# The one-hots of the edge stage made on ScalarE as a clipped distance, in place of VectorE's comparison

## The chip, the cores and the metric

The kernel runs on one core of one Trainium2 chip. The metric is the device time of one execution in microseconds (us), as the median of several runs; less is better. The engines are named as the profile names them: PE is TensorE (matrix products, with PEld for its weight loads), DVE is VectorE, ACT is ScalarE, POOL is GpSimd, SP is SyncE, which only issues DMAs here.

## What is computed

The program is one layer of a graph network on 12,500 nodes with 256 features and 212,500 edges, sorted by their receiving node (`row`). Cut to what matters:

```python
h = relu(layernorm(x))
xn = layernorm(h) * ln_w + ln_b
w_phys = (silu(rbf @ w1 + b1) @ w2 + b2) * cutoff[:, None]
Q, K, V = xn @ wq + bq, xn @ wk + bk, xn @ wv + bv      # 8 heads of 32
q_e, k_e, v_e = Q[row], K[col], V[col]
scores = sum(q_e * k_e, per head) / sqrt(32) * cutoff[:, None]
attn = softmax(scores, axis=1)                          # over the 8 heads of one edge
combined = xn[col] * w_phys + gate * attn * v_e
aggr = segment_sum(combined, row)
out = x + h + aggr @ wo + bo
```

## The kernel before, in words

The program has three stages. The first (`prep`) makes the node tables, sorts the edges into buckets of 128 receiving nodes, computes `w_phys` for each edge and writes one record per edge to memory. The last (`finish`) multiplies the sums by `wo`. Between them stands the edge stage (`edges`), the only place that the change touches.

The edge stage works in **units** of 256 edge slots (two columns j of 128 edges, one edge per partition), UNITS of them, 880 in all. A record (`REC` = 260 floats) holds an edge's 256 weights, its cutoff (`R_CUT`), the number 0 to 127 of its receiving node in its bucket (`R_LOC`) and the number of its sending node (`R_DST`). Buffers for records, gathered rows and one-hots are DEPTH = 8 units deep. For each unit u:

- SP loads the records of unit u (L1010), once the last readers of unit u - 8's buffer are done: `physical`, `weigh` and `select` on VectorE (L1007 to L1009).
- GpSimd gathers the 768 floats (K, V, xn) of each sending node by two indirect DMAs (L1029). It runs GATHER_AHEAD = 5 units ahead in its own count and waits until TensorE has aggregated unit u - 8 and until the record is there.
- VectorE's `select` (L1191) makes the one-hots of two units at once: it compares the column numbers 0 to 127 (`iota_bf`, bf16) with `R_LOC` of each edge. The result `ohb` (`uonehot_bf`) is a matrix of edges by nodes of the bucket, one 1 in each row.
- TensorE's `turn` (L1103) transposes the two one-hots of a unit into PSUM, and ScalarE's `evacuate` (L1046) copies them to `uonehotT` as float32. `query` (L1111) multiplies them by the bucket's queries, which gives each edge its Q row.
- ScalarE's `widen` (L1052) copies `ohb` to float32 (`uonehot`) for the aggregation.
- VectorE multiplies queries by keys (`query_key`, L1198, each unit), weights by xn (`physical`, L1203), reduces over the heads (`score`, L1210), scales (`weigh`, L1215), takes the maximum (`maximum`, L1220), inverts and normalises after ScalarE's exponentials (L1225, L1230), and weighs the values (`attend`, L1236). All of these but `query_key` work on a **pair** of units.
- ScalarE's `exponent` (L1060) makes the four exponentials of a pair.
- TensorE's `aggregate` of unit u - 3 (LAG = 3) multiplies the float32 one-hots by the two products (L1131, L1134) and sums them in PSUM, `renew_next` (L1115) zeroes the next bank, and ScalarE's `keep` (L1070) copies the sums out.

The order of each engine is written out by hand: a function `unit` per engine, called for unit 0, 1, 2 and so on, in which `ahead(fn, n, ...)` issues the step fn of unit u + n. An engine executes its own order strictly; between engines there are only semaphores. VectorE's `unit` in the kernel before, for odd u:

```python
                else:
                    score(u, k, i, first)
                    weigh(u, k, i, first)
                    maximum(u, k, i, first)
                    ahead(select, SELECT_AHEAD - 1, u, k, i, first, last)
```

ScalarE's `unit` issues `evacuate` and `widen` of unit u + 2, for odd u `exponent`, then `keep` of unit u - 3. TensorE's issues `aggregate(u - 3)`, `turn(u + 3)`, `query(u + 2)`, `renew_next(u - 3)`; for even u it first loads bucket numbers into registers.

## Time and profile before

| | |
|---|---|
| median of 3 runs | 5721.61 us (5720.52 to 5729.41) |
| the profiled execution | 5727.87 us |
| its span | 5726.1 us |
| PE busy | 5242.1 us, 92% |
| DVE busy | 4458.7 us, 78% |
| POOL busy | 4114.1 us, 72% |
| ACT busy | 3117.6 us, 54% |
| mean TensorE clock granted | 0.987 of full speed |

A busy time is the sum over the whole span, so it mixes the three stages. The edge stage takes the stretch from about 2590 us to about 5590 us. In it, an engine's idle time before a group of instructions is given with what released it ("<-"); "issue" is time in which it waited for nothing that the profile shows. Matmuls are pipelined and their ends are modelled, so the distance between two starts says more about PE than its busy share.

### The profile page before, as it was taken

What the parts mean: (1) busy time and instruction counts of PE and PEld (TensorE: products, weight loads), DVE (VectorE), ACT (ScalarE), POOL (GpSimd) and SP (SyncE); (2) the same over time, 40 slices, a digit from 0 to 9 for tenths busy, and PEclk for the clock granted to TensorE, in tenths of its full rate; (3) what the DMA queues carried; (4) which work ended last, traced back from release to release, by engine and by line L of the source; (5) the groups of instructions that cost most, each with busy time, mean ns of one, the idle gap of its engine ahead of it and who ended that gap; (6) DMA issues with size and microseconds to landing.
All of it is one profiled execution on the core that took longest, in us unless ns stands there. A gap on an engine that the chain in (4) does not pass through costs nothing. (4 is left out here: it accounts for less than half of the span.)

```text
span 5726.1 us, 115218 instructions
## 1 busy us (share of the span) xinstructions
PE 5242.1 (92%) x24352; PEld 3838.2 (67%) x24353; DVE 4458.7 (78%) x7861; ACT 3117.6 (54%) x9962; POOL 4114.1 (72%) x3476
## 2 busy tenths in 40 slices
PE   3889999999999999996899999999999999999999
PEld 3556666666666666664666666666666666666667
DVE  8889976666655554226899999999999999999995
ACT  4546565666666666563455555555555555555553
POOL 1567777777777777675777777777777777777770
PEclk9989999999999999997999999999999999999999
DMA  6234354444444444438999999999999999999955
GB/s 196 90 109 150 121 169 165 156 134 157 165 155 142 150 166 159 142 125 299 312 307 303 305 308 304 303 305 303 308 305 306 307 307 304 304 306 306 308 185 180
DMA packets 584396, 1306.11 MB, mean 228 GB/s; under 512 B 81246, under 2 KB 384134, under 8 KB 582961
## 3 DMA queue, kind: packets, MB, share of 16 engines
q0 software_dynamic: 221536, 881.08, 44.2%
q1 hardware_dynamic: 311796, 345.48, 20.4%
q10 hardware_dynamic: 50850, 77.03, 3.7%
q8 instruction: 95, 1.56, 0.1%
q14 instruction: 119, 0.97, 0.1%
HBM read 1024.15 MB, written 324.38 MB: 236 GB/s over the span
## 5 line engine op out<-in xcount | busy, mean ns | idle before, releaser
L1029 POOL DMA_INDIRECT ukvx<-kvx_table,urec x1760 | 2302.3, 1308 | 705.0 <-issue 640.5
L339 POOL DMA_INDIRECT records<-rows,slot_i x1660 | 1743.9, 1051 | 682.8 <-issue 468.5
L694 PE MATMUL w_ps<-w2s,hid 128*128 128x256 f32 x6656 | 1553.9, 387 | 51.3 <-DVE rows L608 51.1
L694 PEld LDWEIGHTS w_ps<-w2s,hid 128*128 128x128 f32 x6656 | 1249.9, 193 | 375.3 <-issue 156.5
L608 DVE TENSOR_TENSOR rows<-w_ps,b2b 128x512 f32<-128x512 f32 x832 | 571.3, 687 | 744.1 <-PE w_ps L694 743.9
L1131 PE MATMUL ag_ps<-ukvx,uonehot 128*128 128x256 f32 x3520 | 987.3, 403 | 153.5 <-DVE ukvx L1203 78.2
L1111 PE MATMUL uq_ps<-aggr,uonehotT 128*128 x3520 | 974.9, 400 | 0.3 <-issue 0.3
L808 ACT ACTIVATE hid<-hid_ps,b1t 128x512 f32<-128x512 f32 x832 | 525.4, 682 | 820.9 <-PE hid_ps L683 806.2
L1134 PE MATMUL ag_ps<-ukvx,uonehot 128*128 128x256 f32 x3520 | 906.5, 380 | 1.0 <-DVE ukvx L1236 1.0
L1060 ACT ACTIVATE uexp<-uscores,umax 128x8 f32<-128x8 f32 x1760 | 507.5, 289 | 649.2 <-DVE umax L1220 649.1
L1131 PEld LDWEIGHTS ag_ps<-ukvx,uonehot 128*128 128x128 f32 x3520 | 600.1, 190 | 372.2 <-issue 273.9
L1046 ACT ACTIVATE uonehotT<-turn_ps 128x256 f32<-128x256 bf16 x880 | 328.6, 373 | 831.8 <-PE turn_ps L1103 826.7
L829 ACT ACTIVATE rows<-rows 128x256 f32<-128x256 f32 x1664 | 706.9, 504 | 66.5 <-DVE rows L608 66.3
L1134 PEld LDWEIGHTS ag_ps<-ukvx,uonehot 128*128 128x128 f32 x3520 | 670.9, 191 | 93.6 <-DVE ukvx L1236 1.8
L1111 PEld LDWEIGHTS uq_ps<-aggr,uonehotT 128*128 128x128 f32 x3520 | 601.1, 190 | 90.3 <-issue 0.6
L1198 DVE TENSOR_TENSOR ukvx<-uq_ps,ukvx 128x512 f32<-128x512 f32 x880 | 601.3, 683 | 0.5 <-PE uq_ps L1111 0.5
L1210 DVE TENSOR_REDUCE uscores<-ukvx 128x32 f32<-128x1024 f32 x440 | 536.7, 1220 | 50.5 <-DVE ukvx L1198 20.6
L1236 DVE TENSOR_TENSOR ukvx<-ukvx,uexp 128x1024 f32<-128x1024 f32 x440 | 539.2, 1225 | 45.7
L1203 DVE TENSOR_TENSOR ukvx<-urec,ukvx 128x1024 f32<-128x1024 f32 x440 | 534.6, 1215 | 11.3 <-DMA ukvx<-kvx_table,urec 11.1
L1070 ACT ACTIVATE aggr<-ag_ps x880 | 510.0, 580 | 2.7 <-ACT aggr L1070 1.6
L683 PE MATMUL hid_ps<-rT,w1d 64*128 64x512 f32 x1664 | 472.8, 645 | 26.7 <-ACT hid L808 20.6
L441 DVE TENSOR_TENSOR_SCAN cs_ps<-eq,run 128x512 f32<-128x512 bf16 (+1 forms) x396 | 405.8, 1025 | 28.4 <-DVE run L449 11.1
(174 smaller groups left out, 4629.6 us busy)
## 6 DMA issues: line engine op xcount, KB each, us to landing
urec<-records SPq DMA_DIRECT2D x880, 260.0 KB, 6.3
rbf_in<-in_edge_attr SPq DMA_DIRECT2D x207, 256.0 KB, 3.0
kvx_table<-kvx ACTq DMA_DIRECT2D x10, 3456.0 KB, 14.5
ukvx<-kvx_table,urec POOLq DMA_INDIRECT x1760, 5.9
records<-rows,slot_i POOLq DMA_INDIRECT x1661, 2.1
records<-kvx SPq DMA_DIRECT2D x1, 13000.0 KB
aggr<-query_table SPq DMA_DIRECT2D x7, 1792.0 KB, 20.1
fbase<-x_plus_h SPq DMA_DIRECT2D x14, 896.0 KB, 7.2
```

Source lines behind the costliest of these rows:

```text
L339: pool.indirect_dma_start(recs, bass.IndirectOffsetOnAxis(ap=slot_i[:, q, t:t + 1], axis=0), rows[:, q, t, :], None).then_inc(scattered[q] ...
L608: dve.tensor_tensor(rows[:, q, 2 * j:2 * j + 2, 0:H], w_ps[j % 2][:], b2b[:].unsqueeze(1).to_broadcast([P, 2, H]), ALU.add).then_inc(s["w_ ...
L694: m = pe.matmul(w_ps[j % 2][:, h, :], hid[:, k % 2, c, h, j * P:(j + 1) * P], w2s[:, c, :], start=(h == 0 and c == 0), stop=(c == 1), skip ...
L829: m = act.activation(rows[:, q, t, 0:H], rows[:, q, t, 0:H], ACT.Copy, scale=rows[:, q, t, R_CUT:R_CUT + 1])
L1029: pool.indirect_dma_start(kvx[:, k, j, :], None, table, bass.IndirectOffsetOnAxis(ap=rec[:, k, j, R_DST:R_DST + 1].bitcast(I32), axis=0), ...
L1111: m = pe.matmul(q_ps[k % 3][:, j, :], ohT[:, k % 4, j, :], aggr[:, bass.ds(buckets[j] + QLAG, 1), :].rearrange("p a f -> p (a f)"), start= ...
L1131: pe.matmul(to[j], oh[:, k, j, :], kvx[:, k, j, 2 * H:3 * H], start=False, stop=False, skip_group_check=True)
L1134: m = pe.matmul(to[j], oh[:, k, j, :], kvx[:, k, j, H:2 * H], start=False, stop=(j == 1), skip_group_check=True)
L1198: dve.tensor_tensor(kvx[:, k, :, 0:H], q_ps[k % 3][:], kvx[:, k, :, 0:H], ALU.mult).then_inc(s["qk_done"], 1)
L1203: dve.tensor_tensor(both, pair(rec, k)[:, :, 0:H], both, ALU.mult).then_inc(s["phys_done"], 2)
L1210: dve.tensor_reduce(sc[:, q], pair(kvx, k - 1)[:, :, 0:H].rearrange("p r (h d) -> p r h d", h=NH), AX_X, ALU.add).then_inc(s["scored"], 2)
L1236: dve.tensor_tensor(values, values, ex[:, q].unsqueeze(3).to_broadcast([P, 4, NH, HD]), ALU.mult).then_inc(s["av_done"], 2)
```

## The change

`select` is gone from VectorE. ScalarE makes the one-hots of all units in two steps, in bf16 and in place. `spread` writes the distance |R_LOC - column| with the function Abs (one instruction of 128x128 for each of the two columns j, since the bias is one number per partition). `pick` writes Relu(1 - distance), which is 1 where the distance is 0 and 0 elsewhere (one instruction of 128x256 per unit, its bias from a new tile `one` that VectorE sets once). In ScalarE's `unit`, `spread` of unit u + 5 and `pick` of unit u + 4 stand behind `exponent` and ahead of `keep`. TensorE's `turn`, ScalarE's `widen` and SP's record load wait for the new semaphore `picked` where they waited for `onehot_ready`. At the start ScalarE makes the distances of units 0 to 4 and the one-hots of units 0 to 3 ahead of its first `evacuate`.

```diff
@@ -929,6 +929,7 @@
         kvx = sb("ukvx", [P, DEPTH, 2, TAB])
         iota_bf = sb("uiota_bf", [P, P], BF16)
         ohb = sb("uonehot_bf", [P, DEPTH, 2, P], BF16)
+        one = sb("uone", [P, 1])
         ident_bf = sb("uident_bf", [P, P], BF16)
         oh = sb("uonehot", [P, DEPTH, 2, P])
         ohT = sb("uonehotT", [P, 4, 2, P])
@@ -941,7 +942,7 @@
         ag_ps = ps("ag_ps", [P, SUMS, H])
 
         s = {n: sem("u_" + n) for n in (
-            "zeroed", "narrow", "blank", "rec_waited", "onehot_ready", "widened", "turned", "ohT_ready", "qe_done",
+            "zeroed", "narrow", "blank", "rec_waited", "one_ready", "spread", "picked", "widened", "turned", "ohT_ready", "qe_done",
             "qk_done", "phys_done", "scored", "weighted", "max_done", "exp_ready", "recip_done", "shared",
             "av_done", "ag_waited", "ag_done", "kept", "q_waited", "named")}
         rec_in = [sem(f"u_rec_in{k}") for k in range(DEPTH)]
@@ -949,7 +950,7 @@
         q_in = sem("u_q_in")
         kvx_in = [sem(f"u_kvx_in{k}") for k in range(DEPTH)]
         TURNS = UNITS // DEPTH
-        GATHER_AHEAD, SELECT_AHEAD, TURN_AHEAD, OUT_AHEAD, ASK_AHEAD = 5, 4, 3, 2, 2
+        GATHER_AHEAD, SPREAD_AHEAD, TURN_AHEAD, OUT_AHEAD, ASK_AHEAD = 5, 5, 3, 2, 2
         rec_v = recs.rearrange("(u j p) f -> u p j f", p=P, j=2)
         q_v = queries.rearrange("(b p) f -> p b f", p=P)
 
@@ -1006,7 +1007,7 @@
                 if not first:
                     sp.wait_ge(s["phys_done"], u - (DEPTH - 1))
                     sp.wait_ge(s["weighted"], u - (DEPTH - 1))
-                    sp.wait_ge(s["onehot_ready"], u - (DEPTH - 1))
+                    sp.wait_ge(s["picked"], u - (DEPTH - 1))
                 sp.dma_start(rec[:, k], rec_v[u] if isinstance(u, int) else rec_v[bass.ds(u, 1)].rearrange("a p j f -> p (a j) f")).then_inc(rec_in[k], 16)
                 if first and k == 2:
                     ask_first(0, q_first[0])
@@ -1045,8 +1046,21 @@
                     act.wait_ge(s["qe_done"], u - 3)
                 act.activation(ohT[:, k % 4], turn_ps[:, 0:2, :], ACT.Copy).then_inc(s["ohT_ready"], 1)
 
+            def spread(u, k, i, first):
+                act.wait_ge(rec_in[k], i * 16 + 16)
+                if not first:
+                    act.wait_ge(s["widened"], u - (DEPTH - 1))
+                    act.wait_ge(s["turned"], u - (DEPTH - 1))
+                for j in range(2):
+                    m = act.activation(ohb[:, k, j, :], iota_bf[:], ACT.Abs, scale=-1.0, bias=rec[:, k, j, R_LOC:R_LOC + 1])
+                m.then_inc(s["spread"], 1)
+
+            def pick(u, k, i, first):
+                act.wait_ge(s["spread"], u + 1)
+                act.activation(ohb[:, k], ohb[:, k], ACT.Relu, scale=-1.0, bias=one[:, 0:1]).then_inc(s["picked"], 1)
+
             def widen(u, k, i, first):
-                act.wait_ge(s["onehot_ready"], u + 1)
+                act.wait_ge(s["picked"], u + 1)
                 if not first:
                     act.wait_ge(s["ag_done"], u - (DEPTH - 1))
                 act.activation(oh[:, k], ohb[:, k], ACT.Copy).then_inc(s["widened"], 1)
@@ -1071,6 +1085,12 @@
 
             act.activation(half_asked[:], half_bucket[:, HPAD:HPAD + HALVES], ACT.Copy).then_inc(s["named"], 1)
             bucket_of = [None] * 4
+            act.wait_ge(s["narrow"], 2)
+            act.wait_ge(s["one_ready"], 1)
+            for k in range(SPREAD_AHEAD):
+                spread(k, k, 0, True)
+                if k:
+                    pick(k - 1, k - 1, 0, True)
             for k in range(OUT_AHEAD):
                 evacuate(k, k, 0, True)
                 widen(k, k, 0, True)
@@ -1082,6 +1102,8 @@
                 ahead(widen, OUT_AHEAD, u, k, i, first, last)
                 if k % 2:
                     exponent(u, k, i, first)
+                ahead(spread, SPREAD_AHEAD, u, k, i, first, last)
+                ahead(pick, SPREAD_AHEAD - 1, u, k, i, first, last)
                 if not (first and k < LAG):
                     keep(u - LAG, bucket_of[k % 2 * 2])
             turns(act, unit)
@@ -1096,7 +1118,7 @@
         @block.tensor
         def _(pe):
             def turn(u, k, i, first):
-                pe.wait_ge(s["onehot_ready"], u + 1)
+                pe.wait_ge(s["picked"], u + 1)
                 if not (first and k == 0):
                     pe.wait_ge(s["ohT_ready"], u)
                 for j in range(2):
@@ -1182,15 +1204,6 @@
             def pair(tile, k):
                 return tile[:, k:k + 2].rearrange("p k j e -> p (k j) e")
 
-            def select(u, k, i, first):
-                for n in range(2):
-                    dve.wait_ge(rec_in[k + n], i * 16 + 16)
-                if not first:
-                    dve.wait_ge(s["widened"], u - (DEPTH - 2))
-                    dve.wait_ge(s["turned"], u - (DEPTH - 2))
-                dve.tensor_tensor(pair(ohb, k), iota_bf[:].unsqueeze(1).to_broadcast([P, 4, P]),
-                                  pair(rec, k)[:, :, R_LOC:R_LOC + 1].to_broadcast([P, 4, P]), ALU.is_equal).then_inc(s["onehot_ready"], 2)
-
             def query_key(u, k, i, first):
                 q = k % 2
                 dve.wait_ge(s["qe_done"], u + 1)
@@ -1235,13 +1248,11 @@
                 values = pair(kvx, k - 1)[:, :, H:2 * H].rearrange("p r (h d) -> p r h d", h=NH)
                 dve.tensor_tensor(values, values, ex[:, q].unsqueeze(3).to_broadcast([P, 4, NH, HD]), ALU.mult).then_inc(s["av_done"], 2)
 
+            dve.memset(one[:], 1.0).then_inc(s["one_ready"], 1)
             dve.tensor_copy(ident_bf[:], ident[:]).then_inc(s["narrow"], 1)
             dve.tensor_copy(iota_bf[:], iota1[:]).then_inc(s["narrow"], 1)
             for k in range(GATHER_AHEAD):
                 dve.memset(kvx[:, k], 0.0).then_inc(s["blank"], 1)
-            dve.wait_ge(s["narrow"], 2)
-            for k in range(0, SELECT_AHEAD, 2):
-                select(k, k, 0, True)
             dve.memset(zeros_bf[:], 0.0).then_inc(s["zeroed"], 1)
             dve.memset(ag_ps[:], 0.0).then_inc(s["zeroed"], 1)
             for k in range(GATHER_AHEAD, DEPTH):
@@ -1258,7 +1269,6 @@
                     score(u, k, i, first)
                     weigh(u, k, i, first)
                     maximum(u, k, i, first)
-                    ahead(select, SELECT_AHEAD - 1, u, k, i, first, last)
             turns(dve, unit)
             U = UNITS
             before = (U - 1, DEPTH - 1, TURNS - 1, False)
```

**ScalarE, one odd unit and its neighbour in the steady loop.** Rows are instructions in ScalarE's order; L1052 is `widen`, L1060 the four exponentials, L1070 `keep`. Before:

```order
L1052 ACTIVATE uonehot<-uonehot_bf 128x256
L1056 REGISTER_ALU
L1058 REGISTER_ALU
L1060 ACTIVATE uexp,usum<-uscores,umax 128x8 x4
L1070 REGISTER_ALU x2
L1070 ISA
L1070 REGISTER_ALU
L1070 ISA
L1070 ACTIVATE aggr<-ag_ps 128x512
```

With the change (L1066 is `widen`, L1074 the exponentials, L1055 `spread`, L1060 `pick`, L1084 `keep`):

```order
L1066 ACTIVATE uonehot<-uonehot_bf 128x256
L1070 REGISTER_ALU
L1074 ACTIVATE uexp,usum<-uscores,umax 128x8 x4
L1055 ACTIVATE uonehot_bf<-uiota_bf,urec 128x128 x2
L1059 REGISTER_ALU
L1060 ACTIVATE uonehot_bf<-uonehot_bf,uone 128x256
L1084 REGISTER_ALU x2
L1084 ISA
L1084 REGISTER_ALU
L1084 ISA
L1084 ACTIVATE aggr<-ag_ps 128x512
```

Three instructions stand between the exponentials and `keep`; in an even unit the same three follow `widen` directly.

**VectorE, from the end of one pair to the next, in the steady loop.** L1220 is `maximum`, L1191 `select`, L1198 `query_key`, L1203 `physical`. Before:

```order
L1210 TENSOR_REDUCE uscores<-ukvx 128x32
L1215 SCALAR_TENSOR_TENSOR uscores<-uscores,urec 128x32
L1220 TENSOR_REDUCE umax<-uscores 128x4
L1187 ISA
L1191 TENSOR_TENSOR uonehot_bf<-uiota_bf,urec 128x512
L1196 REGISTER_ALU
L1198 TENSOR_TENSOR ukvx<-uq_ps,ukvx 128x2x256
L1203 TENSOR_TENSOR ukvx<-urec,ukvx 128x4x256
```

With the change (L1233 is `maximum`, L1211 `query_key`, L1216 `physical`):

```order
L1223 TENSOR_REDUCE uscores<-ukvx 128x32
L1228 SCALAR_TENSOR_TENSOR uscores<-uscores,urec 128x32
L1233 TENSOR_REDUCE umax<-uscores 128x4
L1209 REGISTER_ALU
L1211 TENSOR_TENSOR ukvx<-uq_ps,ukvx 128x2x256
L1216 TENSOR_TENSOR ukvx<-urec,ukvx 128x4x256
```

`query_key` of the next unit follows the maximum; nothing else has moved on VectorE.

## Rows read from the trace of the kernel before

**Rows 1.** The page: busy times over the span, and two groups of its part 5.

```profile
PE 5242.1 (92%) x24352; PEld 3838.2 (67%) x24353; DVE 4458.7 (78%) x7861; ACT 3117.6 (54%) x9962; POOL 4114.1 (72%) x3476
...
L829 ACT ACTIVATE rows<-rows 128x256 f32<-128x256 f32 x1664 | 706.9, 504 | 66.5 <-DVE rows L608 66.3
...
L1198 DVE TENSOR_TENSOR ukvx<-uq_ps,ukvx 128x512 f32<-128x512 f32 x880 | 601.3, 683 | 0.5 <-PE uq_ps L1111 0.5
```

**Rows 2.** Stage table: window, length, busy us per engine, clock, DMA share, GB/s.

```profile
4000.00:4500.00 500.00, 457.63 (x2221) 347.77 (x2220) 453.87 (x742) 257.86 (x1037) 390.77 (x297) 1.00 0.92 307
```

**Rows 3.** Instruction groups, window 2700 to 5500 us: busy us, mean ns, idle before.

```profile
L1029 POOL DMA_INDIRECT ukvx<-kvx_table,urec x1658 | 2176.8, 1313 | 625.7 <-issue 600.5 <-PE ag_ps L1134 22.7 <-DMA urec<-records 2.5
L1131 PE MATMUL ag_ps<-ukvx,uonehot 128*128 128x256 f32 x3312 | 926.4, 402 | 147.3 <-DVE ukvx L1203 76.4 <-ACT uonehot L1052 70.8 <-issue 0.2
...
L1198 DVE TENSOR_TENSOR ukvx<-uq_ps,ukvx 128x512 f32<-128x512 f32 x828 | 565.8, 683 | 0.0
...
L1203 DVE TENSOR_TENSOR ukvx<-urec,ukvx 128x1024 f32<-128x1024 f32 x414 | 503.0, 1215 | 4.6 <-DMA ukvx<-kvx_table,urec 4.6
...
L1060 ACT ACTIVATE uexp<-uscores,umax 128x8 f32<-128x8 f32 x1656 | 477.5, 289 | 599.8 <-DVE umax L1220 599.8
...
L1191 DVE TENSOR_TENSOR uonehot_bf<-uiota_bf,urec 128x512 bf16<-128x512 bf16 x414 | 286.5, 692 | 36.7 <-DMA urec<-records 0.2
```

**Rows 4.** Waits, same window: engine, line, releaser; total us, times, longest.

```profile
ACT uonehotT L1046 <- PE turn_ps L1103: 758.3, 415, 3.2
...
PE turn_ps L1103 <- DVE uonehot_bf L1191: 90.4, 309, 2.1
```

**Rows 5.** VectorE's timeline across one boundary of pairs: start us, length us.

```profile
4003.75 0.19 DVE L1220 TENSOR_REDUCE umax<-uscores 128x4 f32<-128x32 f32 x1
4004.08 0.69 DVE L1191 TENSOR_TENSOR uonehot_bf<-uiota_bf,urec 128x512 bf16<-128x512 bf16 x1
4004.69 0.68 DVE L1198 TENSOR_TENSOR ukvx<-uq_ps,ukvx 128x512 f32<-128x512 f32 x1
4005.29 1.22 DVE L1203 TENSOR_TENSOR ukvx<-urec,ukvx 128x1024 f32<-128x1024 f32 x1
```

**Rows 6.** VectorE's timeline in the start of the edge stage.

```profile
2606.58 0.69 DVE L1191 TENSOR_TENSOR uonehot_bf<-uiota_bf,urec 128x512 bf16<-128x512 bf16 x1 [9.16 <-DMA urec<-records]
...
2614.32 0.63 DVE L1198 TENSOR_TENSOR ukvx<-uq_ps,ukvx 128x512 f32<-128x512 f32 x1
```

**Rows 7.** ScalarE's timeline: two exponentials of 8 columns in a row.

```profile
4004.27 0.28 ACT L1060 ACTIVATE uexp<-uscores,umax 128x8 f32<-128x8 f32 x1
...
4004.56 0.28 ACT L1060 ACTIVATE uexp<-uscores,umax 128x8 f32<-128x8 f32 x1
```

**Rows 8.** ScalarE's timeline in the first stage: four instructions of L829 merged.

```profile
1501.18 1.70 ACT L829 ACTIVATE rows<-rows 128x256 f32<-128x256 f32 x4
```

**Rows 9.** TensorE's timeline: the first matmuls of three units in a row.

```profile
3999.62 1.13 PE L1131 MATMUL ag_ps<-ukvx,uonehot 128*128 128x256 f32 x4 [0.22 <-ACT uonehot L1052]
...
4002.50 1.11 PE L1131 MATMUL ag_ps<-ukvx,uonehot 128*128 128x256 f32 x4
...
4006.41 1.12 PE L1131 MATMUL ag_ps<-ukvx,uonehot 128*128 128x256 f32 x4 [0.23 <-ACT uonehot L1052]
```

**Rows 10.** GpSimd's timeline: three gathers in a row.

```profile
4003.93 1.01 POOL L1029 DMA_INDIRECT ukvx<-kvx_table,urec  x1 [0.30 <-issue]
4005.38 2.00 POOL L1029 DMA_INDIRECT ukvx<-kvx_table,urec  x1 [0.44 <-issue]
4007.69 1.41 POOL L1029 DMA_INDIRECT ukvx<-kvx_table,urec  x1 [0.30 <-issue]
```

**Rows 11.** Stage table in short windows, columns as in rows 2.

```profile
4002.00:4004.00 2.00, 2.00 (x11) 1.68 (x11) 1.64 (x4) 0.47 (x3) 1.39 (x3) 1.00 1.08 417
...
2652.00:2660.00 8.00, 5.98 (x31) 4.52 (x30) 5.52 (x9) 3.47 (x14) 6.07 (x6) 1.00 1.02 380
```

**Rows 12.** DMA issues, window 2700 to 5500 us: count, KB each, us to landing.

```profile
urec<-records SPq DMA_DIRECT2D x828, 260.0 KB, 6.3
```

## The prediction

> **What bounds the kernel now.** On the page [rows 1] TensorE is busy 92% of the span and ScalarE 54%, which invites the reading that TensorE is the bound and that ScalarE has room to give. A page adds up three stages, so the next view is the stage table, and in it the edge stage alone [rows 2]: in 500 us VectorE is busy 453.87, TensorE 457.63, GpSimd 390.77, ScalarE 257.86, the clock is at its full level and the DMA engines are at 0.92. Four resources are near their end, so busy shares can't name the one that sets the pace; what an engine waits for can. The groups of the window 2700 to 5500 [rows 3] hold 414 pairs of units, so a pair takes 2800 / 414 = 6.76 us. VectorE's idle time before its instructions is released by nobody else: `query_key` 0.0 us, `physical` 4.6 us on a gather, `select` 36.7 us of which 0.2 us is a DMA. What is left of its idle time is the latency between its own dependent steps. TensorE waits for VectorE (`turn` on `select`, 90.4 us), ScalarE waits 758.3 us for TensorE [rows 4] and 599.8 us for the maximum [rows 3]. All chains lead to VectorE, so **VectorE's own sequence is the bound**, and its length per pair is the time per pair. `query_key` is issued 880 times in all [rows 1], so there are 440 pairs.
>
> **What VectorE loses.** In the timeline [rows 5] `select` starts at 4004.08 and the next `query_key` at 4004.69, so it takes 0.61 us of the sequence (its 0.69 us overlap the next start). Between the end of the maximum (4003.94) and `select` there are 0.14 us; on average this idle is 36.7 / 414 = 0.09 us [rows 3]. Whether it goes too is not to be seen in the trace: `query_key` also has waits of its own to be cleared after the maximum was issued, as `select` had. The ends are 0.61 (the gap stays) and 0.70 (it goes). I take 0.61, since every VectorE step that follows a small reduction shows such a gap. That gives 6.76 - 0.61 = 6.15 us per pair and 440 x 0.61 = **-268 us**; the other end is 440 x 0.70 = -308 us.
>
> **The start of the stage.** VectorE stood 9.16 us in the second `select` until a record had landed, then cleared more buffers, and began `query_key` at 2614.32 [rows 6]. Now ScalarE waits for the records, also for that of unit 4, before its first `evacuate`, while VectorE goes on clearing. One comes earlier and the other later. The ends are -8 us (2614.32 - 2606.58, all of VectorE's clearing goes ahead) and +3 us (the new work of five units, estimated below, comes on top). The first queries are not there much before 2614, so I take 0. The new memset of one column and the two selects of the start lie in the same cover.
>
> **What ScalarE gains.** Per unit two instructions of 128x128 and one of 128x256, each with its bias from SBUF. Four instructions of 128x256 with such an operand take 1.70 us [rows 8] and one takes 0.504 [rows 1], so they follow each other by (1.70 - 0.504) / 3 = 0.40 us. With 8 columns the starts lie 4004.56 - 4004.27 = 0.29 us apart [rows 7] (the read of the accumulator fits into that), so 128 columns lie between 0.29 and 0.40; by columns 0.34. Per pair: 4 x 0.34 + 2 x 0.40 = 2.16 us. ScalarE is busy 257.86 / 500 x 6.76 = 3.49 us per pair now [rows 2], so it comes to 5.65 of 6.15 us. It fits, and it fits because its idle time lies in two waits per pair: before `evacuate` (758.3 / 414 = 1.8 us) and before the exponentials (599.8 / 414 = 1.45 us) [rows 3, 4]. About 1.1 us of new work falls before each. The first 1.1 us use up most of the 1.45 us left before the exponentials, so these start on time. The second 1.1 us delay the `evacuate` behind the exponentials, and with it TensorE's `query` of two units later. VectorE has never waited for a query there (0.0 us [rows 3]), so there is reserve, of unknown size. I cost ScalarE at nothing; without this cover each 0.1 us per pair is 44 us.
>
> The Trainium skill (ScalarE: Activation LUTs, Rules for kernel authors) speaks against this change: relu and the like belong on VectorE, not on ScalarE. Rows 3 agree as to the work, 0.69 us on VectorE against 2.16 us estimated on ScalarE. By that rule the sum would be a loss, which is my rival on the other side; by the rows the cheap engine is the one that is full.
>
> **What TensorE can do.** Without a wait inside, a unit takes 4002.50 - 3999.62 = 2.88 us; the next took 3.91 us [rows 9]. Of the difference, the wait for `select` goes: `pick` of a unit is issued well before its `turn`. The idle time before the first matmul, 147.3 / 414 = 0.36 us per pair [rows 3], comes with the loading of bucket numbers into registers (the releasers named had long been done) and may stay. TensorE's floor is then 2 x 2.88 + 0.36 = 6.12 us, just under VectorE's 6.15. It is late next, by nearly nothing.
>
> **What GpSimd can do.** Its gathers follow each other with gaps of 0.30 to 0.44 us and look like a bound of their own [rows 10]. A gather takes 1.01 us, but 2.00 when it begins with `physical` and 1.41 within `attend`; the mean is 1.313 us [rows 3]. With gaps of 0.30 four gathers take 4 x 1.61 = 6.45 us per pair. But the stretching follows VectorE: a gather that starts inside such an instruction goes on when it ends, so gathers and pairs are locked in phase. In a shorter pair the same gather starts later inside `physical` and loses less. It loses 0.99 us beside `physical` now and needs to lose 6.45 - 6.15 = 0.30 us less. So GpSimd should follow at 6.15 us. If it doesn't, it is the bound at 6.45.
>
> The Trainium skill (SBUF — State Buffer, Who interferes with whom) says that a VectorE instruction with two SBUF inputs contends with a GpSimd instruction that reads SBUF. The two products agree, with 2.00 and 1.41 us against 1.01; `select` has two SBUF inputs as well, and the gather that ran beside it took 1.01 [rows 5, 10]. By that rule GpSimd would regain up to 0.4 us per pair, as much as a gather loses within `attend`, and my rival (a) below would drop out. The row shows nothing to regain, so I leave (a) its chance.
>
> **What the DMA engines can do.** Their share of 0.92 times 6.76 is 6.22 us per pair, if a share of 1 were the limit. But a share holds time in which two queues' packets overlap, and 307 GB/s [rows 2] is not the most: 380 over 8 us, 417 over 2 us [rows 11]. 6.15 us per pair need 307 x 6.76 / 6.15 = 337 GB/s. A record takes 6.3 us to land [rows 12], and under more load longer. I expect a few tenths more, within the distance that SP and GpSimd run ahead.
>
> **The sum.** The profiled execution took 5727.9 us; less 268 that is 5459.9 us. It lies 6.3 us above the median of the runs shown, so the median should be about 5454 us.
>
> **Rivals.** *Another resource at its end, faster by less.* (a) GpSimd holds at 6.45 us per pair: 440 x 0.31 = -136 us, 5586 us. For it: it has no long idle time now. Against it: VectorE almost never waited for a gather, though GpSimd has no reserve to catch up with if it were the slower. Chance 0.17. (b) DMA at a share of 1, 6.22 us: -238 us, 5484 us, or TensorE keeps half of the 1.03 us that its longer unit has over the shorter [rows 9], 2 x 2.88 + 0.52 = 6.28 us: -211 us, 5511 us. Chance 0.13.
>
> *ScalarE becomes the bound, slower.* The mechanism is the strict order on ScalarE behind the exponentials: `spread`, `pick` and `keep` stand ahead of the next `evacuate`, and VectorE's reciprocal waits for the next exponentials. It decides from the point at which the six new instructions of a pair cost more than 6.76 - 3.49 = 3.27 us, 0.55 each. If none overlaps its neighbour and each first waits for a semaphore, they cost up to 0.504 + 0.1 (as between VectorE's dependent steps) = 0.6, 3.6 us per pair, and the pair takes 7.09: 440 x 0.33 = +145 us, 5867 us. Half of that is as likely, 5790 us. Against it: ScalarE's neighbours overlap by 0.1 us wherever the trace shows them, also after a release. Chance 0.09.
>
> *It does not do what it says:* VectorE's pace was set from outside and only looked full, so that the freed 0.61 us turn into a wait for gathers or queries. 5722 us. The 4.6 and 0.0 us of waits [rows 3] speak against it. Chance 0.04.
>
> **How the numbers follow.** VectorE (with TensorE beside it) as the bound at 6.06 to 6.2 us per pair has a chance of 0.57, and gives 5408 to 5480 us. With (b) it is 0.70, with (a) 0.87. The range has to hold 0.8: from 5405 us (the gap goes too, and 3 us of the start) to 5620 us, which takes in (a) with a margin for slower landings. Left out are the slower case, the case of no change and the space between. A measurement of this kernel can tell about 0.2% from no change. Faster by more: 0.57 + 0.13 + 0.17 = 0.87; within: 0.04; slower: 0.09.
>
> **What would show it.** In the groups of the window 2700 to 5500 there should be about 455 pairs. VectorE's `query_key` should still be preceded by no idle time released by others. TensorE's wait for the one-hots should be gone. `spread` should show a mean near 0.39 us and `pick` near 0.50, and ScalarE a busy share near 0.9. The gather's mean should be below 1.313 us, and its waits for TensorE no longer than now. The DMA rate should be near 337 GB/s. I am wrong if `physical` waits for gathers by tenths of a us per pair (then it is (a) or (b)), if the reciprocal waits for the exponentials or `turn` for ScalarE (then it is ScalarE), or if `query_key` waits for the queries (then it is TensorE).

## The result, and the profile after

| | before | with the change |
|---|---|---|
| median | 5725.51 us (4 runs) | 5507.36 us (4 runs, 5505.26 to 5509.57) |
| span of the profiled execution | 5726.1 us | 5503.4 us |
| ratio | | 0.9618, 95% interval 0.9602 to 0.9635 |

The change makes the kernel 3.8% faster, 218 us, where 268 were forecast. The page of the changed kernel, the line that answers to the first of [rows 1]:

```profile
PE 5147.0 (94%) x24352; PEld 3858.7 (70%) x24353; DVE 4196.1 (76%) x7422; ACT 3928.7 (71%) x12602; POOL 3871.3 (70%) x3476
```

VectorE has 262.6 us less to do and ScalarE 811 us more. The stage table, as [rows 2]:

```profile
4000.00:4500.00 500.00, 481.34 (x2409) 382.81 (x2410) 445.92 (x723) 427.61 (x1606) 376.46 (x322) 1.00 0.96 333
```

ScalarE went from 258 to 428 busy us in 500; the DMA rate rose from 307 to 333 GB/s. The groups of the window 2700 to 5300 us (busy us, mean ns, idle before, as [rows 3]; the new lines are L1211 `query_key`, L1216 `physical`, L1055 `spread`, L1060 `pick`, L1074 exponentials, L1030 gathers):

```profile
L1030 POOL DMA_INDIRECT ukvx<-kvx_table,urec x1664 | 1947.4, 1170 | 652.5 <-issue 621.8 <-PE ag_ps L1156 15.9 <-DMA urec<-records 14.8
...
L1211 DVE TENSOR_TENSOR ukvx<-uq_ps,ukvx 128x512 f32<-128x512 f32 x832 | 571.5, 687 | 45.2 <-issue 30.8 <-PE uq_ps L1133 14.3
...
L1055 ACT ACTIVATE uonehot_bf<-uiota_bf,urec 128x128 bf16<-128x128 bf16 x1664 | 566.8, 389 | 5.9 <-DMA urec<-records 5.8
...
L1216 DVE TENSOR_TENSOR ukvx<-urec,ukvx 128x1024 f32<-128x1024 f32 x416 | 506.7, 1218 | 31.3 <-DMA ukvx<-kvx_table,urec 29.0
...
L1074 ACT ACTIVATE uexp<-uscores,umax 128x8 f32<-128x8 f32 x1664 | 479.7, 289 | 374.0 <-DVE umax L1233 371.4 <-issue 2.5
L1060 ACT ACTIVATE uonehot_bf<-uonehot_bf,uone 128x256 bf16<-128x256 bf16 x833 | 413.0, 496 | 0.0
```

416 pairs in 2600 us are 6.25 us per pair, against 6.76 before and 6.15 forecast. `spread` takes 389 ns and `pick` 496, as estimated. The gather's mean fell from 1313 to 1170 ns. VectorE now has idle time that others end: 29.0 us on gathers where it had 4.6, and 14.3 us on queries, of which 14.0 lie before 2800 us.

The mean hides that most pairs (267 of the last 419) are shorter than 6.15 us. VectorE's timeline over two boundaries of pairs (start us, length us):

```profile
4008.31 0.19 DVE L1233 TENSOR_REDUCE umax<-uscores 128x4 f32<-128x32 f32 x1
4008.49 0.69 DVE L1211 TENSOR_TENSOR ukvx<-uq_ps,ukvx 128x512 f32<-128x512 f32 x1
...
4014.43 0.19 DVE L1233 TENSOR_REDUCE umax<-uscores 128x4 f32<-128x32 f32 x1
4014.92 0.69 DVE L1211 TENSOR_TENSOR ukvx<-uq_ps,ukvx 128x512 f32<-128x512 f32 x1 [0.31 <-issue]
```

At an ordinary boundary the gap between the maximum and `select` (0.14 us in [rows 5]) went together with `select`: `query_key` starts where the maximum ends. At one boundary in four, where VectorE's loop of 8 units turns (jumps back to its start), 0.31 us stand open instead. Taking the distance between the starts of every second `query_key` over the whole stage, the medians of the four pairs of a loop turn are

| us per pair (medians) | 1st | 2nd | 3rd | 4th | mean of all pairs after the 20th |
|---|---|---|---|---|---|
| before | 6.86 | 6.68 | 6.78 | 6.68 | 6.751 |
| with the change | 6.13 | 6.03 | 6.03 | 6.38 | 6.217 |

The first 20 pairs took 154.2 us before and 164.3 us after, so they gained nothing. These three things, the longer fourth pair, the difference between the mean and the medians, and the slow start, are what the experiments take apart.

### The profile page after: what moved, and what is told of

Its sections match the earlier page's. It is cut to its first block and busy times, and to the rows that moved or that the text cites. A ratio compares the mean times of both kernels' runs of the same rounds, so it can differ in the third digit from the quotient of the medians.

```text
span 5503.4 us, 117739 instructions
## 1 busy us (share of the span) xinstructions
PE 5147.0 (94%) x24352; PEld 3858.7 (70%) x24353; DVE 4196.1 (76%) x7422; ACT 3928.7 (71%) x12602; POOL 3871.3 (70%) x3476
## 5 line engine op out<-in xcount | busy, mean ns | idle before, releaser
L1030 POOL DMA_INDIRECT ukvx<-kvx_table,urec x1760 | 2058.7, 1170 | 737.6 <-issue 663.6
L1133 PE MATMUL uq_ps<-aggr,uonehotT 128*128 x3520 | 976.9, 400 | 88.4 <-issue 72.7
L1074 ACT ACTIVATE uexp<-uscores,umax 128x8 f32<-128x8 f32 x1760 | 507.3, 289 | 402.2 <-DVE umax L1233 399.7
L829 ACT ACTIVATE rows<-rows 128x256 f32<-128x256 f32 x1664 | 706.7, 504 | 66.7 <-DVE rows L608 66.7
L1133 PEld LDWEIGHTS uq_ps<-aggr,uonehotT 128*128 128x128 f32 x3520 | 602.4, 191 | 206.1 <-issue 155.2
L1211 DVE TENSOR_TENSOR ukvx<-uq_ps,ukvx 128x512 f32<-128x512 f32 x880 | 604.5, 687 | 76.1 <-PE uq_ps L1133 44.5
L1055 ACT ACTIVATE uonehot_bf<-uiota_bf,urec 128x128 bf16<-128x128 bf16 x1760 | 599.6, 389 | 43.3 <-DMA urec<-records 43.1
L1216 DVE TENSOR_TENSOR ukvx<-urec,ukvx 128x1024 f32<-128x1024 f32 x440 | 535.9, 1218 | 36.9 <-DMA ukvx<-kvx_table,urec 34.7
L1084 ACT ACTIVATE aggr<-ag_ps x880 | 508.6, 578 | 2.3 <-ACT aggr L1084 1.6
L1060 ACT ACTIVATE uonehot_bf<-uonehot_bf,uone 128x256 bf16<-128x256 bf16 x880 | 436.3, 496 | 0.0
```

Source lines behind the costliest of these rows:

```text
L829: m = act.activation(rows[:, q, t, 0:H], rows[:, q, t, 0:H], ACT.Copy, scale=rows[:, q, t, R_CUT:R_CUT + 1])
L1030: pool.indirect_dma_start(kvx[:, k, j, :], None, table, bass.IndirectOffsetOnAxis(ap=rec[:, k, j, R_DST:R_DST + 1].bitcast(I32), axis=0), ...
L1055: m = act.activation(ohb[:, k, j, :], iota_bf[:], ACT.Abs, scale=-1.0, bias=rec[:, k, j, R_LOC:R_LOC + 1])
L1133: m = pe.matmul(q_ps[k % 3][:, j, :], ohT[:, k % 4, j, :], aggr[:, bass.ds(buckets[j] + QLAG, 1), :].rearrange("p a f -> p (a f)"), start= ...
L1211: dve.tensor_tensor(kvx[:, k, :, 0:H], q_ps[k % 3][:], kvx[:, k, :, 0:H], ALU.mult).then_inc(s["qk_done"], 1)
```

## The experiments

All ratios are against the kernel before. The last two columns come from the one profiled execution of each kernel. Two executions of the same code can reach the edge stage some us apart (VectorE's first instruction of the stage came at 2579.8 us in the profile of the changed kernel, at 2588.5 in that of the kernel before and at 2592.7 in another, although the change does not touch what stands ahead). Differences below 10 us between medians are therefore read with the times inside the stage.

| kernel | median us | ratio (95% interval) | first 20 pairs us | mean of the rest us |
|---|---|---|---|---|
| changed kernel | 5507.4 | 0.9618 (0.9602 to 0.9635) | 164.3 | 6.217 |
| e_compare_back | 5667.6 | 0.9892 (0.9876 to 0.9909) | 166.9 | 6.575 |
| e_free_act | 5471.7 | 0.9559 (0.9543 to 0.9575) | 145.0 | 6.167 |
| e_half_records | 5497.8 | 0.9599 (0.9583 to 0.9615) | 160.2 | 6.195 |
| e_half_query | 5504.9 | 0.9605 (0.9589 to 0.9621) | 159.0 | 6.217 |
| e_all_light | 5458.4 | 0.9527 (0.9513 to 0.9542) | 143.2 | 6.136 |
| e_free_records | 5456.1 | 0.9529 (0.9515 to 0.9544) | 144.2 | 6.132 |
| e_busy_act | 5493.9 | 0.9591 (0.9577 to 0.9606) | 147.0 | 6.222 |
| e_act_beside | 5730.6 | 1.0005 (0.9996 to 1.0015) | 154.8 | 6.754 |
| e_keep_first | 5508.8 | 0.9615 (0.9600 to 0.9630) | 166.3 | 6.222 |
| e_spread_later | 5504.4 | 0.9608 (0.9594 to 0.9623) | 155.4 | 6.241 |
| e_branch_moved | 5488.2 | 0.9582 (0.9569 to 0.9595) | 164.8 | 6.169 |
| e_branch_load | 5476.9 | 0.9568 (0.9555 to 0.9581) | 159.5 | 6.163 |

### VectorE's comparison back, as work that nobody waits for

```diff
+            def compare(u, k, i, first):
+                dve.tensor_tensor(spare[:].rearrange("p k j e -> p (k j) e"), iota_bf[:].unsqueeze(1).to_broadcast([P, 4, P]),
+                                  marks[:].to_broadcast([P, 4, P]), ALU.is_equal)
...
                     maximum(u, k, i, first)
+                    compare(u, k, i, first)
```

> The changed kernel with VectorE's comparison back as work that nobody waits for: the same 128x512 bf16 instruction into a spare tile, from a constant, behind the maximum. If VectorE's sequence sets the pace, the pair gets 0.61 us back at least (to 6.64) and the time is 5507 + 0.53 to 0.61 x 440 = 5740 to 5775, or 5715 if the register-free form leaves a part of the gap out and slack elsewhere absorbs some. If TensorE or ScalarE had become the bound, less than half of it returns: below 5640.

It returned 160 us, less than the theory that it should confirm had said, and a little more than the other theory's bound. VectorE's timeline of this kernel says why (L1239 is the maximum, L1210 the comparison, L1217 `query_key`):

```profile
4006.51 0.18 DVE L1239 TENSOR_REDUCE umax<-uscores 128x4 f32<-128x32 f32 x1
4006.61 0.68 DVE L1210 TENSOR_TENSOR uspare<-uiota_bf,umarks 128x512 bf16<-128x512 bf16 x1
4007.21 0.68 DVE L1217 TENSOR_TENSOR ukvx<-uq_ps,ukvx 128x512 f32<-128x512 f32 x1
```

The comparison without waits starts 0.10 us after the start of the maximum and overlaps it by 0.08 us, so the gap of the kernel before is not there. `select` had four semaphore waits and read the record; the comparison has no wait and reads a constant. Which of the two made the gap no run separates. An ordinary pair takes 6.54 us by the medians, 0.51 more than 6.03. The fourth takes 6.54 too, only 0.16 more than 6.38: the comparison covers the open 0.31 us there. And the scatter is gone: in the changed kernel 47 pairs after the 20th are over 6% above the median and add 33 us, here one. VectorE's sequence sets the pace of nearly every pair in both kernels; the other disturbances show in the changed kernel and no longer when VectorE's own pair is about 0.5 us longer.

The same timeline shows what the comparison does to a gather that begins inside it:

```profile
4006.69 1.48 POOL L1032 DMA_INDIRECT ukvx<-kvx_table,urec  x1 [0.30 <-issue]
```

It takes 1.48 us in place of 1.01 (297 gathers begin inside it in the window 2700 to 5300 and take 1.47 us on average). In the kernel before `select` did the same:

```profile
4017.62 0.69 DVE L1191 TENSOR_TENSOR uonehot_bf<-uiota_bf,urec 128x512 bf16<-128x512 bf16 x1
...
4017.86 1.33 POOL L1029 DMA_INDIRECT ukvx<-kvx_table,urec  x1 [0.30 <-issue]
```

### The three suspects relieved, one by one and together

ScalarE unburdened: one-hots are made in the first turn of 8 units only, so later units use those of other edges.

```diff
-                ahead(spread, SPREAD_AHEAD, u, k, i, first, last)
-                ahead(pick, SPREAD_AHEAD - 1, u, k, i, first, last)
+                if first and k < DEPTH - SPREAD_AHEAD:
+                    spread(u + SPREAD_AHEAD, k + SPREAD_AHEAD, 0, True)
+                if first and k < DEPTH - SPREAD_AHEAD + 1:
+                    pick(u + SPREAD_AHEAD - 1, k + SPREAD_AHEAD - 1, 0, True)
...
-                pe.wait_ge(s["picked"], u + 1)
+                pe.wait_ge(s["picked"], u + 1 if first else DEPTH)
```

`widen` waits like `turn`, and the record load no longer waits for `picked`.

> The changed kernel, with ScalarE's spread and pick only in the first turn of 8 units; later units use those one-hots again, so the one-hots of all later units are not those of their edges. VectorE as changed, ScalarE unburdened as before the change. Records theory (VectorE paces at 6.03 us per pair, and what is missing to 6.03 is records and gathers that land late): within 15 us of the changed kernel's 5507. ScalarE theory (its 2 us of new work per pair delay the evacuations, and TensorE's turn and query behind them): 5400 to 5440. TensorE theory (tied with VectorE, its own register loads cost in each fourth pair): 5495 to 5507.

-36 us against the changed kernel, between the two forecasts. In the profile the first 20 pairs fall from 164.3 to 145.0 us and the rest from 6.217 to 6.167 us per pair (21 us).

Shorter records: from the second turn on the first 128 of the 256 weights are not loaded.

```diff
+                lo = 0 if first else H // 2
...
+                sp.dma_start(rec[:, k, :, lo:REC], src[:, :, lo:REC]).then_inc(rec_in[k], 16)
```

> The changed kernel, but from the second turn on the record load leaves out the first 128 of the 256 weights (260 floats become 132), so the physical product uses old weights there. DMA work per pair falls by 0.26 MB of 2.1 MB and records land sooner. Records theory: the disturbed pairs (some 0.09 us per pair) and the slow first 20 pairs (43 us over 6.03 each) mostly go, 5507 becomes 5425 to 5460. ScalarE and TensorE theories: 5495 to 5507.

-10 us, far less than the records theory had said. Late records alone are not all that is missing.

TensorE relieved: after the first turn only half of each unit's query products.

```diff
-                for j in range(2):
+                for j in range(2 if first else 1):
                     m = pe.matmul(q_ps[k % 3]
```

> The changed kernel, but after the first turn query multiplies only the first 128 edges of each unit, so the other half uses old query rows. TensorE saves about 0.85 us per pair. TensorE theory: each fourth pair falls from 6.38 to about 6.1 us and disturbed pairs are caught up sooner, 5460 to 5480. Records theory: 5490 to 5507, since VectorE's chain is as long. ScalarE theory: 5495 to 5507.

No difference that can be told, and the fourth pair stays at 6.34 us. Neither the pace nor the longer fourth pair comes from TensorE's query products.

All three together:

> The changed kernel with all three reliefs together: one-hots only in the first turn, half the weights loaded, half the query products (outputs are not the reference's). Only VectorE's own chain is left at its full length: 4 pairs in 6.13 + 6.03 + 6.03 + 6.34, 6.13 on average, 440 x 6.13 = 2697 us and about 2690 + 26 us from the start of the stage: about 80 us under the changed kernel's 2799, 5425 to 5440. Above 5450 something else holds VectorE that none of the three touches.

5458.4 us. The time was 18 us above the range and the pairs were as expected: 6.136 us on average against the 6.13 of the four medians, so nothing holds VectorE up after the start, and only the start's 143 us (20 x 6.13 would be 123) were more than I had allowed. What holds VectorE up there, none of the three reliefs shows. The first two reliefs without the third:

> The changed kernel with two of the three reliefs of the earlier run (one-hots only in the first turn, half the weights loaded), the query products whole. If TensorE has no part in what is missing to VectorE's chain: 5455 to 5463, as with all three (5458). If it has: 5467 to 5472, as with ScalarE relieved alone.

5456.1 us, as with all three, so TensorE's query products have no part in it. VectorE's `physical` in this kernel, window 2700 to 5300:

```profile
L1219 DVE TENSOR_TENSOR ukvx<-urec,ukvx 128x1024 f32<-128x1024 f32 x423 | 514.1, 1215 | 5.7 <-DMA ukvx<-kvx_table,urec 5.7
```

VectorE's wait for gathers is back at 5.7 us, where ScalarE's relief alone had left 13.5 and the changed kernel has 29.0. So the account is: from 5726 to 5456 us for VectorE's shorter sequence with everything else out of its way, 270 us; given back 36 us for ScalarE, and 16 us while the full records load beside it (51 us in all).

### What of ScalarE costs: its wait for records, or its being full

e_busy_act takes the kernel with one-hots in the first turn only and puts three instructions of the same kinds and sizes in place of `spread` and `pick` in every later unit, from a constant tile, with a wait for their own predecessors but for no record.

```diff
+            def beside(u, k, i):
+                act.wait_ge(s["beside"], u * 3 - (DEPTH * 3 - 3))
+                for j in range(2):
+                    act.activation(spare[:, j, :], ramp[:, j, :], ACT.Abs, scale=-1.0, bias=one[:, 0:1]).then_inc(s["beside"], 1)
+                act.activation(spare2[:], ramp[:], ACT.Relu, scale=-1.0, bias=one[:, 0:1]).then_inc(s["beside"], 1)
```

> The kernel with one-hots only in the first turn, plus on ScalarE in every later unit the three instructions of spread and pick at their place, from a constant tile into spare tiles: ScalarE is as full as in the changed kernel, but waits for no record. (One-hots of later units are not those of their edges.) Head-of-line theory (the 36 us between the changed kernel and ScalarE unburdened come from its wait for records ahead of the next evacuation): 5465 to 5480. Occupation theory (they come from ScalarE being 0.85 busy, so that a late pair isn't caught up): 5500 to 5512.

Neither theory alone: 5493.9 us, 22 us above ScalarE unburdened and 14 below the changed kernel. The two halves lie at different places. The first 20 pairs take 147.0 us, as with ScalarE unburdened (145.0); the rest takes 6.222 us per pair, as in the changed kernel (6.217). So at the start it is the wait for records, and from then on it is ScalarE being full. (The profiled execution of this kernel is the slowest of its four, 10 us above the median; the two columns are from it.) In the later part VectorE waits longer for gathers, not for queries. Its waits in the window 2800 to 5300 (total us, times, longest):

```profile
DVE ukvx L1229 <- DMA ukvx<-kvx_table,urec: 26.0, 51, 1.8
```

This wait is 8.6 us with ScalarE unburdened and 24.3 us in the changed kernel; for queries VectorE waits under 1 us in all three. The chain at the start can be read in the changed kernel's timeline (L1055 `spread`, L1125 `turn`, L1133 `query`, L1211 `query_key`):

```profile
2628.91 0.69 ACT L1055 ACTIVATE uonehot_bf<-uiota_bf,urec 128x128 bf16<-128x128 bf16 x2 [11.34 <-DMA urec<-records]
...
2630.38 0.37 ACT L1047 ACTIVATE uonehotT<-turn_ps 128x256 f32<-128x256 bf16 x1
...
2630.89 0.37 PE L1125 MATMUL turn_ps<-uident_bf,uonehot_bf 128*128 128x128 bf16 x2 [9.82 <-ACT uonehotT L1047]
...
2631.53 2.07 PE L1133 MATMUL uq_ps<-aggr,uonehotT 128*128 x4 [0.26 <-issue]
...
2633.63 0.69 DVE L1211 TENSOR_TENSOR ukvx<-uq_ps,ukvx 128x512 f32<-128x512 f32 x1 [11.39 <-PE uq_ps L1133]
```

A record for five units ahead is late, ScalarE stands 11.34 us in `spread`, the evacuation of three units ahead stands behind it although its input is long there, TensorE waits 9.82 us for the evacuation, and VectorE 11.39 us for the queries. In the kernel before, `select` asked for the same record later in the order, and ScalarE never stood for one.

The same three instructions beside the kernel before, with `select` in place:

> The kernel before with VectorE's select as it was and on ScalarE the same three instructions per unit as work that nobody waits for. If ScalarE's idle time covers 2 us per pair at 6.75 us per pair: the kernel before's time within 8 us, so 5720 to 5737. If the occupation of ScalarE costs by itself: 5745 or more.

A ratio of 1.0005, and 6.754 us per pair against 6.751. ScalarE was 396 us busy in 500 there:

```profile
4000.00:4500.00 500.00, 458.00 (x2222) 347.98 (x2221) 453.84 (x741) 395.65 (x1480) 391.01 (x297) 1.00 0.92 306
```

So 2 us of new work per pair on ScalarE cost nothing at 6.75 us per pair, and 22 us in all at 6.2 us. The idle time before the exponentials is the reserve that differs: with this work it is 1.36 us per pair at 6.75, and 374.0 / 416 = 0.90 us in the changed kernel. It may be that a pair that comes late for another reason is caught up by less in each of the next pairs. That this is how it acts is an inference from the two runs, and how a full ScalarE makes gathers late is not shown: the profile names no releaser for most of GpSimd's idle time.

### Two other orders on ScalarE

`spread` and `pick` behind `keep` in place of ahead of it:

```diff
-                ahead(spread, SPREAD_AHEAD, u, k, i, first, last)
-                ahead(pick, SPREAD_AHEAD - 1, u, k, i, first, last)
                 if not (first and k < LAG):
                     keep(u - LAG, bucket_of[k % 2 * 2])
+                ahead(spread, SPREAD_AHEAD, u, k, i, first, last)
+                ahead(pick, SPREAD_AHEAD - 1, u, k, i, first, last)
```

> The changed kernel with spread and pick behind keep in ScalarE's unit in place of ahead of it. The record's arrival then holds back the evacuation only, no longer the keep. If keep behind late one-hots were part of the loss: 5490 or less. Head-of-line theory (the evacuation of unit u+3 behind the wait for record u+5 is what costs, and it stays behind it here): 5500 to 5512.

Nothing changes (5508.8 us), as the head-of-line theory had it: it is not `keep` behind `spread` that matters. That leaves the evacuation, and the `widen` behind it.

`spread` four units ahead in place of five (`SPREAD_AHEAD` 4, with `pick` of the same unit right behind it):

> The changed kernel with spread only 4 units ahead in place of 5, and pick directly behind it, so ScalarE asks for each record one unit (3 us) later, but waits once more for its own result in each unit. Head-of-line theory: ScalarE's waits for records at the start of the stage (28 us in the first 160 us) shrink, and so does the slow start (20 pairs in 164 us): 5475 to 5495. If ScalarE's occupation alone is what costs, the added wait makes it worse: 5510 to 5540.

5504.4 us, within neither range and no difference that can be told. It has both effects: the first 20 pairs take 155.4 us, 9 less, and the rest 6.241 us per pair, 10 us more in all. ScalarE's idle time before the exponentials falls by half:

```profile
ACT uexp L1074 <- DVE umax L1232: 179.8, 398, 1.8
```

This is from its waits in the window 2800 to 5300 us. `pick` now waits for `spread` to end before each start.

### The longer fourth pair

VectorE's steps in the same order, but its loop turns behind `query_key` of unit 0 in place of ahead of it:

```diff
             def unit(u, k, i, first, last):
-                query_key(u, k, i, first)
                 if k % 2 == 0:
...
                     maximum(u, k, i, first)
-            turns(dve, unit)
+                ahead(query_key, 1, u, k, i, first, last)
+            query_key(0, 0, 0, True)
+            turns(dve, unit)
```

> The changed kernel, with VectorE's steps in the same order but the loop turning (once in four pairs) after query_key of unit 0 in place of before it, so that 0.69 us of work runs while the branch is taken. Branch theory (the comparison used to run while the loop turned; without it 0.31 us per turn lie open before query_key): each fourth pair falls from 6.34 to about 6.05 us, and 107 turns x 0.3 = 30 us go: 5470 to 5485. If the longer fourth pair comes from TensorE or from late gathers: 5500 to 5510.

5488.2 us, 19 less than the changed kernel; the intervals of the two ratios (0.9569 to 0.9595, 0.9602 to 0.9635) don't touch. The fourth pair falls from 6.38 to 6.07 us. In the groups of the window 2700 to 5300 the 30.8 us of "issue" before `query_key` are gone:

```profile
L1211 DVE TENSOR_TENSOR ukvx<-uq_ps,ukvx 128x512 f32<-128x512 f32 x837 | 576.0, 688 | 17.3 <-PE uq_ps L1133 14.3
```

In the kernel before the loop turned behind `select`, whose 0.69 us covered it: between `select` and `query_key` there is no idle time at that boundary either.

```profile
4010.76 0.69 DVE L1191 TENSOR_TENSOR uonehot_bf<-uiota_bf,urec 128x512 bf16<-128x512 bf16 x1
...
4011.37 0.69 DVE L1198 TENSOR_TENSOR ukvx<-uq_ps,ukvx 128x512 f32<-128x512 f32 x1
```

With `select` gone it turned behind the maximum, 0.19 us long. The measured gain is a little under the 22 to 37 us expected; in the profile it is 0.048 us per pair, 20 us.

With, in addition, TensorE's second load of bucket numbers at the head of an even unit:

```diff
+                    if not first and not (last and k + ASK_AHEAD >= DEPTH):
+                        asking[:] = four(half_asked, u * 2 + 2 * ASK_AHEAD, mybir.EngineType.PE)
...
-                    if k % 2 == 0:
+                    if k % 2 == 0 and first:
                         asking[:] =
```

> The changed kernel with VectorE's loop turning behind query_key, and in addition TensorE's second load of bucket numbers placed behind the first at the head of an even unit, in place of between turn and query, where TensorE stood 0.45 us. A version meant to beat both. If TensorE's stall before query delays late pairs: 5475 to 5485. If VectorE's chain alone sets the pace and TensorE has reserve: as with the loop moved alone, 5485 to 5491.

5476.9 us, the fastest version that computes the whole result: ratio 0.9568, 4.3% under the kernel before and clearly under the changed one. Against e_branch_moved it is 11 us better, but the intervals (0.9555 to 0.9581 and 0.9569 to 0.9595) overlap. In the profiles the first 20 pairs are 5 us shorter and the rest 0.006 us per pair, 3 us in all, and its profiled execution is the slowest of its five. Whether the earlier load brings anything stays open.

## Why the prediction was right, and where it was off

The direction, the bound and the order of size were right; 5507.4 us lies in the range, 53 us above the forecast. By the steps:

**"VectorE's own sequence is the bound."** Shown. With the other resources relieved the pairs run at VectorE's own medians (6.132 us, nothing more), and an unused comparison put back into its sequence costs 160 us.

**"It takes 0.61 us of the sequence ... The ends are 0.61 and 0.70."** The sum was right by luck, out of two errors that cancel. At the three ordinary boundaries the gap did go: the medians fall by 0.73, 0.65 and 0.75 us, 0.71 on average, which is the other end, 0.70. At every fourth, the turn of VectorE's loop, which `select` had covered, stands open, and only 0.30 us are gained. The medians of the four pairs average 6.75 before and 6.14 after: 0.61. With everything else out of VectorE's way it was 5726 - 5456 = 270 us, against the 268 of the forecast. I had read that "every VectorE step that follows a small reduction shows such a gap"; those steps wait for the reduction, and `query_key` doesn't. And the row that I read (0.14 us) was the largest of four: over the stage the median gap before `select` is 0.12, 0.04, 0.14 and 0.04 us at the four boundaries of a turn.

**"I cost ScalarE at nothing."** This is the step that failed: 36 of the 51 us that were given back. The durations were right (0.39 and 0.50 us), the busy time a little less than forecast (5.65 us per pair forecast, 427.61 / 500 x 6.25 = 5.35 measured), and in the steady state ScalarE still has 0.90 us per pair left before the exponentials. But an engine that is 0.86 full costs 22 us in the median even where its new work waits for no record and nobody waits for it, and the strict order that I had priced only as occupation also holds a wait: `spread` for a record of five units ahead stands in front of the evacuation of three ahead (14 us in the median, 17 us in the first 20 pairs of the profile). My rival named that order, but priced it by the length of the instructions, not by a wait. The sign that I had set for ScalarE shows too: `turn` waits 17.6 us for ScalarE's `evacuate` in the window 2700 to 5300.

**"I expect a few tenths more, within the distance that SP and GpSimd run ahead."** Nearly. The DMA rate rose to 333 GB/s (337 forecast), and VectorE's wait for gathers from 4.6 to 29.0 us. Relieving the records on top of ScalarE is worth 16 us, which is the rest of what was given back. The wait is 0.07 us per pair, under the tenths that were to decide for (a) or (b).

**"The start of the stage ... I take 0."** VectorE's first `query_key` came 25.8 us before (2614.32 - 2588.48) and 26.2 us after the stage began (2605.99 - 2579.77): nothing, as taken. What the start costs comes in the 20 pairs behind it. The lower end of the range was to hold 308 us and 3 us of the start; from 5722 that is 5411, not 5405.

**"TensorE's floor is 6.12 us ... late next."** Too high. Pairs of 6.03 us are common, and half of the query products left out changes nothing, so TensorE has reserve.

**"GpSimd should follow."** It did, against rival (a): the gather's mean fell to 1170 ns with the number of gathers unchanged. Most of that is phase: in the window 2700 to 5300 273 gathers began in the first 0.3 us of `physical` before, 20 with the change. But I had misread one row. The gather in [rows 10] that took 1.01 us "beside `select`" began 0.15 us before it. 103 gathers of the kernel before began inside `select` and took 1.34 us on average. They account for 0.02 of the 0.14 us by which the mean fell, so there was something to regain beside `select`, 0.09 us per pair.

**The signs.** TensorE's wait for the one-hots is nearly gone, as foreseen: its matmuls wait 0 us where it was 90.4, its weight loads 20.2 us in 13 waits where it was 247.4. The window 2700 to 5500 could not hold 455 pairs: there are 440 in all, and the last `query_key` starts at 5379 us. The window 2700 to 5300 holds 416 pairs.

## What to carry to other kernels

Taking work off the pacing engine brought its whole share in the sequence. Take that share from several rows, not from one: here the sum from one row was good to 1% because two errors cancelled. Most of what was given back (36 of 51 us) was on the engine that took the work over. Price there not only the busy time but which wait the new step brings into a strict order, and what stands behind it: here a step that looks ahead for its input stood in front of what the other engines wait for, and cost 14 us. And look at what the removed instruction had covered, here a loop's branch, which cost 20 us until other work was put over it.

## What the runs showed that I had not expected

A gather that begins inside a VectorE instruction with two inputs in SBUF (`physical`, `attend`, `select`, the comparison put back) goes on until about 0.88 us after that instruction's end. With 1.08 us of the instruction left it takes 1.95 us, with 0.53 left 1.41, with 0.46 left 1.34 (means over the window 2700 to 5300 of the kernel before). A gather that begins anywhere else, also inside `query_key` or `score`, takes 1.01 us. So GpSimd adapts in phase to VectorE: in both kernels the profile names another engine or a DMA for few of its gaps (25 us in 2800 before, 31 us in 2600 after), the mean gap is 0.38 and 0.39 us, and four gathers take 6.76 us before and 6.25 after. A row of gathers without waits between them can thus be no bound at all.

A VectorE instruction that waits for semaphores starts later than one without, even when what it waits for is long there: behind the maximum `select`, with four waits, stood 0.04 to 0.14 us, `query_key` with two starts 0.01 us before the maximum's end, and the comparison without waits 0.08 us before it. That the waits make the difference is the likely reading; the instructions differ in their inputs too.

The turn of VectorE's loop costs 0.31 us of idle time behind an instruction of 0.19 us, and none behind one of 0.69.
